# Decoder layer, 2048 tokens, one core: queries turned two heads at a time in full precision, with high and low parts made from the turned bank

## What is computed

```python
q = xn @ Wq.T
k, v = (kv[..., :DIM_HEAD], kv[..., DIM_HEAD:])        # kv = xn @ Wkv.T
q, k = (l2norm(q * SCALE), l2norm(k))
sim = jnp.einsum('bhid,bjd->bhij', q * 4, k * 4)       # then the causal mask
attn = jax.nn.softmax(sim)
out = jnp.einsum('bhij,bjd->bhid', attn, v)            # then Wout and a layernorm
```

## Time and profile before

| what | value |
|---|---|
| median of 3 runs | 1018.17 us (1015.82 to 1018.6) |
| profiled execution, time | 1011.42 us |
| its span | 1009.6 us |
| granted clock of TensorE, mean | 0.954 |
| TensorE busy | 883.6 us, 88% of the span |
| VectorE, ScalarE, GpSimd busy | 586.9, 579.6, 198.0 us |
| lead-in, attention stage, rest | 0 to 34.9, 34.9 to 709, 709 to 1009.6 us |

### The profile page before, as it was taken

One profiled execution on the slowest core, in us unless ns is written; L12 is line 12 of the kernel. 1 busy time (PEld: TensorE's weight loads), 2 busy tenths in 40 slices (PEclk: granted clock), 3 DMA queues, 4 the chain that ended last, 5 costly groups with the idle time before them and its releaser, 6 DMA issues.

```text
span 1009.6 us, 14608 instructions
## 1 busy us (share of the span) xinstructions
PE 883.6 (88%) x4510; PEld 675.2 (67%) x4510; DVE 586.9 (58%) x1369; ACT 579.6 (57%) x1144; POOL 198.0 (20%) x220
## 2 busy tenths in 40 slices
PE   3789889999999998888999999999741199999997
PEld 2566667777777766666776777776630178888885
DVE  4456668767676667667677676848576222323331
ACT  2567758677778775667677787878432022222221
POOL 3122222211121112222111111101103401111111
PEclk9799999999999999999999999999975599999999
DMA  8400000000000000000000000000373201010000
GB/s 277 73 1 0 2 1 1 1 1 1 1 1 1 1 0 1 1 1 1 2 1 1 1 1 1 1 1 1 126 265 118 102 1 32 19 32 22 27 21 10
DMA packets 19177, 29.04 MB, mean 29 GB/s; under 512 B 2079, under 2 KB 15648, under 8 KB 19104
## 3 DMA queue, kind: packets, MB, share of 16 engines
q1 hardware_dynamic: 17008, 22.73, 7.5%
q0 software_dynamic: 1680, 4.21, 1.2%
q10 hardware_dynamic: 416, 1.18, 0.3%
...
## 4 chain that ended last, share of the span: by engine, by line
PE 41%; DVE 4%; issue 3%; POOL 2%; DMA 1%; ACT 1%; DVEq 0%; POOLq 0%; ACTq 0%
PE W L1308 7%; PE S L1285 6%; PE O L1285 5%; PE O L1125 3%; PE S L1106 2%; PE S L1107 2%; PE O L1122 2%; PE O L1123 2%; PE W L1196 2%; POOL sorted_rows L595 2%; PE W L1238 1%; PE W L1164 1%; PE W L1218 1%; PE W L1296 1%; PE S L1296 1%
## 5 line engine op out<-in xcount | busy, mean ns | idle before, releaser
L845 DVE TENSOR_TENSOR pl<-pr,ph 128x512 fp32r<-128x512 f32 x288 | 197.5, 689 | 83.1 <-ACT pr L637 65.5
L636 ACT ACTIVATE ph<-S 128x512 fp32r<-128x512 f32 x288 | 174.1, 605 | 120.5 <-PE S L1107 115.6
L637 ACT ACTIVATE pr<-S 128x512 f32<-128x512 f32 x288 | 173.1, 601 | 0.0
L1122 PE MATMUL O<-ph,vhi 128*65 128x512 f32 x288 | 139.7, 485 | 0.0
L1125 PE MATMUL O<-pl,vhi 128*65 128x512 f32 x288 | 114.8, 398 | 9.0 <-DVE pl L845 8.7
L1106 PE MATMUL S<-qT,kT 128*128 128x512 f32 x288 | 114.2, 397 | 0.2 <-ACT kT L676 0.2
L1107 PE MATMUL S<-qT,kT 128*128 128x512 f32 x288 | 113.9, 395 | 0.0
L1123 PE MATMUL O<-ph,vlo 128*65 128x512 f32 x288 | 113.3, 393 | 0.0
L559 POOL TENSOR_TENSOR rn<-ssc,half 128x17 f32<-128x17 f32 x16 | 53.7, 3354 | 150.3 <-DVE ssc L876 150.3
L548 POOL TENSOR_TENSOR rs<-ri,half 128x1 f32<-128x1 f32 x48 | 38.2, 795 | 216.1 <-DVE ri L783 216.1
L753 ACT ACTIVATE gate<-S 128x512 f32<-128x512 f32 x38 | 20.6, 595 | 103.4 <-PE S L1285 103.4
...
## 6 DMA issues: line engine op xcount, KB each, us to landing
...
```

Source lines behind the costliest of these rows:

```text
L636: nc.scalar.activation(ph[:, k % RING, :], S[k % AHEAD][:], ACT.Exp, scale=SIM_SCALE).then_inc(ph_ready, 1)
L637: nc.scalar.activation(pr[:, k % RING, :], S[k % AHEAD][:], ACT.Exp, scale=SIM_SCALE)\
L845: nc.vector.tensor_tensor(pl[:, k % RING, :], pr[:, k % RING, :], ph[:, k % RING, :].bitcast(F32), ALU.subtract).then_inc(pl_ready, 1)
L1122: nc.tensor.matmul(o, vhi[:, vs, 0:DH + 1], ph[:, k % RING, :], start=j == 0, stop=False)
```

## The change

A transpose now takes two whole heads of `qn` (fp32, 128 columns) instead of one head's two parts. The turned bank holds the even heads on partitions 0 to 63 and the odd ones on 64 to 127. ScalarE copies each half, rounded, to its place in `qT`; VectorE subtracts this from the bank and writes the low part to the other half of the partitions, so that heads again have high and low on the two halves (for odd heads the other way up, which the doubled key doesn't mind). `q_high`, `qhl` and two of the five `q_turn` parts are gone; `k_double` (VectorE) doubles the key before it is turned, `v_parts` (GpSimd) makes the value's parts from `qn`. A bank of `q_turn` is now free when `q_low` has read it. The `q_turn` stages move to earlier places in the slot (7, 11, 14 instead of 11 to 20), each with its `q_low` one place later; `lows_early` moves a `q_low` forward where a third job after its `q_turn` would otherwise come first.

```diff
 STAGES = [
     ("heads_out", 3, -1, 1), ("probs_turn", 0, -3, 1), ("q_norm", 0, 1, 2), ("probs_turn", 1, -3, 2),
-    ("z2_turn", 0, -2, 3), ("q_norm", 1, 1, 3), ("out_turn", 0, -1, 3), ("probs_turn", 2, -3, 4), ("q_high", 0, 1, 4),
-    ("q_low", 0, 1, 5), ("out_turn", 1, -1, 5), ("q_high", 1, 1, 5), ("q_low", 1, 1, 7), ("xq", 0, -2, 6),
+    ("z2_turn", 0, -2, 3), ("q_norm", 1, 1, 3), ("out_turn", 0, -1, 3), ("probs_turn", 2, -3, 4), 
+    ("out_turn", 1, -1, 5), ("xq", 0, -2, 6), ("k_double", 0, 1, 4), ("v_parts", 0, 1, 5), ("q_turn", 0, 1, 7), ("q_low", 0, 1, 8),
+    ("q_turn", 1, 1, 11), ("q_low", 1, 1, 12), ("q_turn", 2, 1, 14), ("q_low", 2, 1, 15),
...
-    ("scores", 0, -2, 10), ("z_turn", 0, 2, 11), ("q_turn", 0, 1, 11), ("xa_norm", 0, -1, 11),
...
 READER = {
-    "kv": ["dve"] * 4, "z_turn": ["act"], "qkv": ["act"] * 3, "q_turn": ["act"] * 5,
+    "kv": ["dve"] * 4, "z_turn": ["act"], "qkv": ["act"] * 3, "q_turn": ["dve"] * 3,
...
+def lows_early(here):
+
+    owed = []
+    for stages in here:
+        n = 0
+        while n < len(stages):
+            name, part, t = stages[n]
+            if name in READER:
+                for entry in owed:
+                    entry[1] += 1
+                for key, _ in [entry for entry in owed if entry[1] >= WB]:
+                    for later in here:
+                        if key in later:
+                            later.remove(key)
+                    n = stages.index((name, part, t))
+                    stages.insert(n, key)
+                    n += 1
+                owed = [entry for entry in owed if entry[1] < WB]
+                if name == "q_turn":
+                    owed.append([("q_low", part, t), 0])
+            elif name == "q_low":
+                owed = [entry for entry in owed if entry[0] != (name, part, t)]
+            n += 1
...
+    def fill(name, part, t):
+
+        if name == "q_low":
+            counts["dve"] += 1
+            freed[turned[part, t]] = ("dve", counts["dve"])
...
             return None
+        if name == "q_turn":
+
+            turned[part, t] = len(freed)
+            freed.append(None)
+            return len(freed) - 1
...
+        def halves_of(part):
+
+            return [(slice(DH * n, DH * (n + 1)), slice(8 * part + n, 8 * part + 8, 2)) for n in range(2)]
...
-                    elif name == "q_low" and part == 1:
-
-                        pool.wait_ge(qhi_ready, 2 * t + 2)
-                        pool.wait_ge(qlo_ready, 2 * t + 2)
+                    elif name == "v_parts":
+
+                        pool.wait_ge(qn_ready, 2 * t + 2)
                         if t >= KV:
                             pool.wait_ge(pv_done, group_start[GROUPS * TPB * ((t - KV) // TPB + 1)])
                         vs = t % KV
-                        nc.gpsimd.tensor_copy(vhi[:, vs, 0:DH], qhl[:, HEADS + 1, 0, :].bitcast(F32)).then_inc(v_ready, 1)
-                        nc.gpsimd.tensor_copy(vlo[:, vs, 0:DH], qhl[:, HEADS + 1, 1, :].bitcast(F32)).then_inc(v_ready, 1)
+                        nc.gpsimd.tensor_copy(vhi[:, vs, 0:DH], qn[:, HEADS + 1, :]).then_inc(v_ready, 1)
+                        pool.wait_ge(v_ready, 2 * t + 1)
+                        nc.gpsimd.tensor_tensor(vlo[:, vs, 0:DH], qn[:, HEADS + 1, :], vhi[:, vs, 0:DH].bitcast(F32),
+                                                ALU.subtract).then_inc(v_ready, 1)
...
-                    elif name == "q_high":
-                        act.wait_ge(qn_ready, 2 * t + part + 1)
-                        if t >= 1:
-                            act.wait_ge(side_ready, job_count("q_turn", 4, t - 1))
-                            act.wait_ge(v_ready, 2 * t)
-                            act.wait_ge(kdup_ready, t)
-                        nc.scalar.copy(qhl[:, part * QH:(part + 1) * QH, 0, :], qn[:, part * QH:(part + 1) * QH, :])\
-                            .then_inc(qhi_ready, 1)
-                    elif name == "q_turn" and part < 4:
+                    elif name == "q_turn" and part < 2:
                         act.wait_ge(side_ready, job + 1)
                         if t >= 2:
                             act.wait_ge(s_ready, group_start[GROUPS * (t - 1)])
-                        nc.scalar.copy(qT[t % 2][:, 4 * part:4 * part + 4, :].rearrange("p h q -> p (h q)"),
-                                       W[job % WB][:]).then_inc(act_freed, 1)
-                    elif name == "q_turn" and part == 4:
+                        for rows, heads in halves_of(part):
+                            nc.scalar.copy(qT[t % 2][rows, heads, :], W[job % WB][rows, :].rearrange("p (h q) -> p h q", q=P))\
+                                .then_inc(qth_ready, 1)
+                    elif name == "q_turn" and part == 2:
                         act.wait_ge(side_ready, job + 1)
                         if t >= KV:
                             act.wait_ge(s_ready, group_start[GROUPS * TPB * ((t - KV) // TPB + 1)])
-                        nc.scalar.copy(kT[:, t % KV].rearrange("p a k -> p (a k)"), W[job % WB][:, 0:2 * P])\
-                            .then_inc(act_freed, 1)
+                        nc.scalar.copy(kT[:, t % KV, 0, :], W[job % WB][:, 0:P]).then_inc(qth_ready, 1)
...
                         if t >= 1:
-                            dve.wait_ge(qhi_ready, 2 * t)
-                            dve.wait_ge(qlo_ready, 2 * t)
+                            dve.wait_ge(side_ready, job_count("q_turn", 1, t - 1))
+                            dve.wait_ge(v_ready, 2 * t)
                         nc.vector.tensor_tensor(qn[:, heads, :], qraw[:].rearrange("p (h d) -> p h d", d=DH)[:, heads, :],
                                                 rn[:, heads].unsqueeze(2).broadcast_to([P, QH, DH]), ALU.mult)\
                             .then_inc(qn_ready, 1)
+                    elif name == "k_double":
+                        dve.wait_ge(qn_ready, 2 * t + 2)
+                        if t >= 1:
+                            dve.wait_ge(side_ready, job_count("q_turn", 2, t - 1))
+                        nc.vector.tensor_copy(kdup[:], qn[:, HEADS, :].unsqueeze(1).broadcast_to([P, 2, DH])).then_inc(kdup_ready, 1)
                     elif name == "q_low":
-                        heads = slice(part * QH, (part + 1) * QH)
-                        dve.wait_ge(qhi_ready, 2 * t + part + 1)
-                        nc.vector.tensor_tensor(qhl[:, heads, 1, :], qn[:, heads, :], qhl[:, heads, 0, :].bitcast(F32),
-                                                ALU.subtract).then_inc(qlo_ready, 1)
-                        if part == 1:
-                            dve.wait_ge(qlo_ready, 2 * t + 2)
-                            nc.vector.tensor_copy(kdup[:], qhl[:, HEADS].bitcast(F32).unsqueeze(2).broadcast_to([P, 2, 2, DH]))\
-                                .then_inc(kdup_ready, 1)
+                        bank = W[job_of["q_turn", part, t] % WB]
+                        if part < 2:
+                            for n, (rows, heads) in enumerate(halves_of(part)):
+                                other = slice(DH, P) if n == 0 else slice(0, DH)
+                                dve.wait_ge(qth_ready, 5 * t + 2 * part + n + 1)
+                                low = nc.vector.tensor_tensor(qT[t % 2][other, heads, :],
+                                                              bank[rows, :].rearrange("p (h q) -> p h q", q=P),
+                                                              qT[t % 2][rows, heads, :].bitcast(F32), ALU.subtract)
+                                low.then_inc(dve_freed if n else qtl_ready, 1)
+                        else:
+                            dve.wait_ge(qth_ready, 5 * t + 5)
+                            nc.vector.tensor_tensor(kT[:, t % KV, 1, :], bank[:, 0:P], kT[:, t % KV, 0, :].bitcast(F32),
+                                                    ALU.subtract).then_inc(dve_freed, 1)
...
-                    pe.wait_ge(act_freed, freed_count("q_turn", 4, t))
+                    pe.wait_ge(dve_freed, freed_count("q_turn", 2, t))
+                    pe.wait_ge(qtl_ready, 2 * (t + 1))
...
                     elif name == "q_turn":
-                        pe.wait_ge(qlo_ready, 2 * t + 2)
-                        pe.wait_ge(kdup_ready, t + 1)
+                        pe.wait_ge(qn_ready, 2 * t + (2 if part else 1))
+                        if part == 2:
+                            pe.wait_ge(kdup_ready, t + 1)
                         freed_wait(pe, job)
-                        for h in range(4 if part < 4 else 2):
-                            src = qhl[:, 4 * part + h].bitcast(F32) if part < 4 else kdup[:, h]
-                            mm = nc.tensor.transpose(W[job % WB][:, h * P:(h + 1) * P], src.rearrange("p a d -> p (a d)"),
-                                                     ident[:])
+                        for c in range(4 if part < 2 else 1):
```

(2 more changed lines are left out.)

23 lines of the change are left out of this document (12 added, 11 removed).

## The result

The kernel after takes 1009.04 us in the median (1004.97 to 1012.65, 8 runs) against 1017.50 us (1014.48 to 1018.60, 8 runs) before: ratio 0.9922, 95% interval 0.9895 to 0.9949. That is 8.5 us less where 13.6 were forecast. A second measurement gave 1006.81 against 1015.68 (6 and 25 runs), ratio 0.9918 (0.9893 to 0.9943). The change makes the kernel faster, inside the range of 998 to 1013, at 60 to 65% of the size forecast.

A forecast was written before the change was run, and what follows sets the result against it. TensorE's queue was taken to set the pace of the attention stage. Transposes 13.9 plus lead-in and first slot 4.5 less new waits 4.8 gave 13.6 us less: 1018.2 to 1004.6 us, range 998 to 1013.

The forecast's parts named there:

- The subtraction's 0.69 us: VectorE, attention: each of the four new 64x512 subtractions a tile, with one operand in PSUM, takes 0.69 us.
- the 0.75 us among the signs of being wrong: VectorE, attention: a subtraction of 64x512 well over 0.75 us would show the prediction wrong.
- half eaten: Rival, short slots: TensorE arrives earlier at the same waits, 7 us more lost; 6.6 us gain, 1011.6 us; chance 0.18.
- 10 to 17 us less: Whole kernel: the forecast's own case, a time 10 to 17 us less than before, given 0.50.
- under 0.8: Long tiles 4 to 7: becoming shorter by less than 0.8 us each would show the prediction wrong.
- The rival of a VectorE held by ScalarE: `q_low` in short slots: VectorE stands up to 2 us, `pl` behind it; at 1.5 us a slot, 1022 us; chance 0.09.
- the term of 4.5 us: Lead-in and slot of tile 0: transposes start earlier, so the projection does; 2.5 and some 2 us, together 4.5 less.
- the 2.5: Lead-in: the projection starts at about 27.9 instead of 30.6 us, taken as 2.5 us gained.
- The new waits for the subtraction: Slots 0 to 3 and 8 to 11: banks held longer cost 0.4 + 0.2 us each, 4.8 us in sum.
- A granted clock under 1.00 behind 215 us: Behind 215 us: a granted clock under 1.00 there would show the prediction wrong.
- 13.9 were counted: TensorE, tiles 2 to 15: nine fewer transposes a tile at 0.11 us each, 13.9 us less.
- the premise that a microsecond off TensorE's queue is nearly one off the span: Short tiles: each microsecond taken from TensorE's queue shortens the span by nearly as much, unless new waits come; 0.99 us a slot.

The follow-up runs named there:

- pad: The kernel after with each transpose of `q_turn` issued twice, so that the 144 taken out are back; 1019.8 us, ratio 1.0037 to the kernel before.
- early1: The kernel after with the `q_turn` stages and their subtractions one place earlier (6, 10, 13 and 7, 11, 14); 1033.3 us.
- after_again: The kernel after, unchanged, run once more beside the experiments; 1006.8 us, ratio 0.9918 to the kernel before.
- before_tuned: The kernel before with spare matmuls (results overwritten) in its waits of TensorE in the attention, and those of tuned2 behind it; 1005.2 us.
- tuned2: The kernel after with spare matmuls (results overwritten) in waits of TensorE, eleven in slot 9 and 46 before the first sorted rows among them; 997.2 us.

## Why the prediction was right, and where it was not

**Right: the bound and the direction.** The attention stage is set by TensorE's queue, and its transposes are worth most of what was counted: pad puts 13.0 us back, 10.5 at one clock. The subtraction's 0.69 us and VectorE's 21 us more (23 forecast) hold too; the 0.75 us among the signs of being wrong comes from no run, and none has such a subtraction at that length (a mean of 688 or 689 ns in all ten that take it out of a bank). TensorE's busy time fell by 9.7 us, not 12 to 16; the kernel after had 10.2 us more of low time in its attention, three stretches that add some 1.5 us of busy time each.

**Luck.** That the range held is the merit of its width, which took in the rival "half eaten"; the forecast's own 10 to 17 us less did not hold. And 2 to 4.5 of the 8.9 us between the medians go with a clock that no term was for.

**Right in four long slots of seven.** Slots 4, 6, 7 and 12 are 1.4, 1.0, 1.0 and 1.5 us shorter. Slots 5 and 13 gained 0.1 and slot 14 0.5; in slot 5 a sign of being wrong that the prediction named (under 0.8) came. The seven gained 5.5 us together of the 6.9 counted. In 5 and 13 something held TensorE; the kernel after, slot 5, in order of time:

```profile
230.83 1.18 ACT L704 CAST qT<-W 64x512 fp32r<-64x512 f32 x2
231.44 1.41 DVE L930 TENSOR_TENSOR qT<-W,qT 64x512 fp32r<-64x512 f32 x2 [1.26 <-ACT qT L704]
232.04 0.37 ACT L686 COPY zT<-W 128x256 f32<-128x256 f32 x1
...
234.11 1.29 DVE L878 TENSOR_TENSOR pl<-pr,ph 128x512 fp32r<-128x512 f32 x2 [0.24 <-ACT ph L677]
234.86 0.44 PE L1169 MATMUL O<-pl,vhi 128*65 128x512 f32 x1 [0.75 <-DVE pl L878]
```

VectorE stands 1.26 us for the cast, `mx` and `sc` follow, ScalarE has two casts and `zT` ahead of its exponentials, and `pl` comes 0.75 us late for TensorE. The rival of a VectorE held by ScalarE is real: the hold is 1.26 us and costs TensorE 0.75, but that is in two slots, not in fifteen. That this is the cause rests on the trace; early1, meant to part the stages, brought waits of its own (slots 5 and 13 at 52.9 and 51.9 us) and doesn't decide it. Why slot 14 gained only half stays open.

**Wrong: the lead-in and the first slot**, the term of 4.5 us. The kernel after, TensorE in order of time, where the earlier trace rows had the transposes at 27.16 and the projection at 30.58:

```profile
23.77 1.97 PE L1218 MATMUL W<-ident,qn 128*128 128x128 f32 x8 [3.71 <-DVE qn L916]
25.53 0.63 PE L1201 MATMUL W<-ident,z 128*128 128x128 f32 x2
27.09 0.45 PE L1218 MATMUL W<-ident,kdup 128*128 128x128 f32 x1 [0.93 <-DVE qT L930]
28.53 5.52 PE L1208 MATMUL W<-wqkv,zT 128*128 128x384 f32 x12 [0.99 <-DVE qT L930]
33.60 0.69 PE L1148 MATMUL S<-below_r,ident_r 128*128 128x512 f32 x1
```

The projection starts 2.05 us earlier, 0.5 short of the count (1.4 us earlier in after_again). The step that failed is the next: that the twelve matmuls of the projection keep their length. Before, the transposes filled the last of the time at half clock (it ended at 31.7) and the projection ran mostly at the full clock; now TensorE stands still twice for a bank, the clock comes back at 31.4 all the same, and the projection runs half its time at half clock. From its start to the first scores it is 5.1 us instead of 4.3, and 0.5 to 1.3 us were left of the 2.5. The slot of tile 0 repeats it: its projection starts at 45.87 us instead of 48.84, as early as forecast and more, but its first four matmuls, at half clock, take 2.90 us instead of 1.50, and the slot is 0.6 us longer (0.9 shorter in after_again, which has one stretch less there than before). The pair at full clock says that even without this there is nothing: in before_tuned 16 transposes take 2.00 us (26.59 to 28.6) and the first scores stand at 32.3, in tuned2 at 33.2. tuned2's own four spare matmuls, behind a bank wait, hold its projection up by 1.0 us (28.66 to 29.65); without them the two would be about level. The volume there was cheap and the two bank waits (0.93 and 0.99) cost as much as it gave.

**Wrong: what short slots keep.** The new waits for the subtraction are 5.9 us against 4.8 forecast, but not where they were put: they stand in slots 0, 1 and 8 (with 1.9 more in the lead-in, counted above). In slots 9 to 11 there is none, and no stretch of half clock in after_again or before, and the 3 us of transposes are lost anyway: the three slots take 118.8 us, 118.5 before. Waits of TensorE in these three slots of after_again, and in those of the kernel before:

```profile
PE W L1232 <- DVE on L947: 6.7, 3, 3.4
PE W L1262 <- DVE on L947: 1.8, 3, 1.1
...
PE W L1262 <- DVE sc L976: 0.9, 2, 0.5
```

```profile
PE W L1188 <- DVE on L904: 6.2, 3, 3.0
...
PE W L1218 <- DVE on L904: 1.2, 3, 0.6
PE W L1218 <- DVE sc L933: 0.5, 1, 0.5
```

All waits there add up to 12.1 us after and 9.8 before (with the rows left out here), while TensorE's busy time fell by 2.0 us, from 108.6 to 106.6: TensorE comes earlier to the same results of VectorE. This is the rival "half eaten", in mechanism; its 3 to 10 us less held the result, at a chance of 0.18, where the forecast's 10 to 17 had 0.50. The measured 1009.0 lies between its 1011.6 and the forecast's 1004.6.

**Missing: the clock.** The sum had no term for it in the slots behind that of tile 0. The earlier trace rows show 1.00 behind 214.7 us; the two stretches that the kernel before had between 55 and 215 us, at 65.8 and 123.8, were not counted either. In their profiled executions the kernel after has two or three stretches of 3.4 us in slots 8 and 10, 1.1 to 1.6 us each, and the kernel before none. "A granted clock under 1.00 behind 215 us" was named as a sign of being wrong, and it came. And the 6.8 us between the profiled execution and the median were carried over to both kernels alike, while they were mostly the clock of one lucky execution of before (0.954 against 0.947, at about 0.8 us for 0.001); the profiled execution of after stands 3.1 us under its median. Between the medians the clock works the other way, for the kernel after.

**The sum again**, for the profiled executions of before and after_again, first scores to the end of the attention:

```profile
34.90:709.50 674.60, 638.32 (x3326) 473.62 (x3325) 464.41 (x1044) 492.91 (x989) 132.62 (x134) 0.99 0.00 1
```

```profile
34.40:704.80 670.40, 628.53 (x3191) 459.11 (x3190) 484.23 (x1089) 479.26 (x959) 140.18 (x134) 0.98 0.00 1
```

TensorE is busy 9.8 us less where 13.9 were counted; two more stretches of half clock, at the 1.5 us of busy time each that slot 1 shows, account for about 3 of the difference. It is idle 5.6 us more (36.3 before, 41.9 after) where 4.8 were counted, in other places than forecast. The lead-in is 0.5 us shorter where it and the first slot were to give 4.5. 9.8 - 5.6 + 0.5 is 4.7, and that is what the attention ends earlier. So two terms of the sum failed: the 4.5 us of the lead-in and the first slot, and, in the short slots, the premise that a microsecond off TensorE's queue is nearly one off the span.
